# Alternating two blocks' DVE chains between the layers of a two-layer graph network, with the second layer's tables moved to the end of the stage

## What is computed

```python
h = relu(layernorm(x));  x = x + L0_gnn(h, ...)      # 12500 nodes x 160, 212500 edges
h = relu(layernorm(x));  x = x + L1_gnn(h, ...)

# layer 0, end of it: messages summed per node into agg (449 columns, one of them a count)
cnt   = clip(segment_sum(1, dst), 1)
alpha = mean(scal) @ Wa * a * inv96
conv  = [mean(scal) @ Wl2_s, mean(vec) @ Wl2_v] * a * inv96
x     = x + sc + alpha * conv
# layer 1, start of it
h     = relu(layernorm(x))
f, skip = h @ W_nl, h @ W_skip          # features gathered by edge, and a skip path
w     = relu(edge_feature @ W_fc1) @ W_fc2   # one row per edge, 224 columns
sh    = edge_attr / |edge_attr|
# then: gather f by dst, multiply, segment_sum by src, W_out, gate, add
```

## Time and profile before

| what | value |
|---|---|
| median of 3 runs | 9630.93 us (9630.51 to 9639.42) |
| the profiled execution | 9623.72 us |
| its span, first to last instruction | 9622.0 us |
| `middle`, first PE instruction to the next stage's first | 6302.34 to 6991.42 us of the span |
| whole span, busy | PE 72%, DVE 75%, ACT 51%, POOL 72% |

### The profile page before, as it was taken

How to read it: one execution, slowest core, us unless ns; L and a number is a source line. 1 busy time by engine, 2 the same in 40 slices (tenths; PEclk the granted TensorE clock), 3 DMA queues, 4 the chain that set the end, 5 groups by cost and what they waited for, 6 DMA issues and landing times. The chain is left out here.

```text
span 9622.0 us, 170670 instructions
## 1 busy us (share of the span) xinstructions
PE 6909.3 (72%) x31166; PEld 4531.3 (47%) x31166; DVE 7250.6 (75%) x21188; ACT 4950.1 (51%) x16490; POOL 6942.6 (72%) x7069
## 2 busy tenths in 40 slices
PE   5666666655666666666666666668789999999999
PEld 3333333332222222222222222245578888888889
DVE  7565665665777777777777777777789999999995
ACT  3444444443444444444444444434467777777774
POOL 4777777777777777777777777756677777777770
PEclk8655555567888888888888888888899999999999
DMA  2222222224444444444444444445456666666667
GB/s 90 92 92 92 92 91 92 92 90 124 138 138 136 137 138 137 137 136 135 138 137 137 137 138 138 130 138 158 153 159 168 169 168 167 168 171 167 170 166 210
DMA packets 826473, 1315.62 MB, mean 137 GB/s; under 512 B 228520, under 2 KB 627624, under 8 KB 826280
## 3 DMA queue, kind: packets, MB, share of 16 engines
q0 software_dynamic: 337920, 667.48, 24.7%
q1 hardware_dynamic: 417496, 547.30, 18.8%
q10 hardware_dynamic: 70992, 100.14, 3.0%
HBM read 862.45 MB, written 914.08 MB: 185 GB/s over the span
## 5 line engine op out<-in xcount | busy, mean ns | idle before, releaser
L1445 POOL DMA_INDIRECT feat_m<-feat_tab,rows_m x3712 | 3653.1, 984 | 1155.3 <-issue 997.9
L1578 ACT ACTIVATE prod_m<-part_m,rows_m 128x64 f32<-128x64 f32 x5568 | 1432.4, 337 | 2197.5 <-DVE part_m L1768 2141.2
L1545 PE MATMUL pair<-prod_m,hot_m 128*128 128x160 f32 x14848 | 2243.5, 304 | 159.2 <-DVE prod_m L1751 119.7
L1545 PEld LDWEIGHTS pair<-prod_m,hot_m 128*128 128x128 f32 x14848 | 2043.4, 190 | 359.4 <-issue 358.2
L1522 PE MATMUL bank<-prod_m,hot_m 128*128 128x449 f32 x2476 | 1424.3, 709 | 944.6 <-DVE prod_m L1788 795.7
L1566 ACT ACTIVATE hot_m<-hot_m,rows_m 128x128 f32<-128x128 f32 x5568 | 1728.7, 389 | 693.1 <-DVE hot_m L1734 687.9
L652 POOL DMA_INDIRECT sorted_rows<-rows_e,place_e x1664 | 1614.4, 970 | 532.1 <-issue 505.2
L1464 POOL DMA_INDIRECT sorted_rows<-later_m,place_m x1248 | 1262.4, 1012 | 380.4 <-issue 345.3
L1522 PEld LDWEIGHTS bank<-prod_m,hot_m 128*128 128x128 f32 x2476 | 542.7, 241 | 1840.1 <-issue 1629.0
L1751 DVE TENSOR_TENSOR prod_m<-rows_m,feat_m 128x192 f32<-128x192 f32 (+2 forms) x4640 | 1316.4, 323 | 0.0
L1768 DVE TENSOR_TENSOR part_m<-rows_m,feat_m 128x128 f32<-128x128 f32 x928 | 271.1, 292 | 1015.1 <-DMA feat_m<-feat_tab,rows_m 1012.1
(11 more groups left out here) (250 smaller groups left out, 10209.4 us busy)
## 6 DMA issues: line engine op xcount, KB each, us to landing
agg_tab<-acc_m ACTq DMA_DIRECT2D x928, 320.0 KB
rows_m<-sorted_rows SPq DMA_DIRECT2D x928, 229.0 KB
agg_tab<-acc_m ACTq DMA_DIRECT2D x928, 224.5 KB
rows_m<-sorted_rows SPq DMA_DIRECT2D x928, 197.0 KB
feat_m<-feat_tab,rows_m POOLq DMA_INDIRECT x3712
turned_m<-in_turned ACTq DMA_DIRECT2D x159, 256.0 KB
agg_s<-agg_tab SPq DMA_DIRECT2D x98, 320.0 KB, 3.3
sorted_rows<-rows_e,place_e POOLq DMA_INDIRECT x1664, 2.4
```

Source lines behind the costliest of these rows:

```text
L1445: pool.indirect_dma_start(out=feat[s % RING][:, k, :], out_offset=None, in_=g.feat_tab[l.n], in_offset=bass.IndirectOffsetOnAxis(ap=rows[s ...
L1545: mm = pe.matmul(dst, hot[s % l.hot_bufs][:, k, q, :], rhs, start=(k == 0 and col == 0), stop=(k == ST_TILES - 1), skip_group_check=True)
L1578: ins = act.activation(prod[s % prods][:, k, at:at + S0], part[s % 2][:, k, 0:S0], ACT.Copy, scale=rows[s % HELD][:, k, l.sh_at + m:l.sh_a ...
```

## The change

DVE's chain is cut into its links. `add_conv` and `node_stats` are split into `count`, `count_inverse`, `count_scale`, `alpha`, `add_conv` (block of one step back) and `stats`, `aggregate`, `positive` (now of two steps back), and a step issues them in turn. What follows from the statistics comes a step later on every engine: `inverse_root`, `root`, `node_turn`, `node_move`, `node_product`, `finish` and the stores (`BLOCK_LAG` 5 to 6). The tables are made after the last step, and PE waits there until the PSUM banks are free. No instruction is added or taken away apart from waits; the buffers are the same.

```diff
-BLOCK_LAG = 5
+BLOCK_LAG = 6
...
 # tensor
             hidden(0, 0)
-            tables_pe(pe, x, g)
...
-                behind(2, node_turn)(step, it, s)
-                behind(3, node_product)(step, it, s)
+                behind(3, node_turn)(step, it, s)
+                behind(4, node_product)(step, it, s)
             turns(pe, MID_STEPS, DEEP, step_, upto=FULL // DEEP)
+            pe.wait_ge(evicted, MID * 4)
+            pe.wait_ge(x_done, NBLK)
+            pe.wait_ge(feat_ready, NBLK)
+            tables_pe(pe, x, g)
...
 # scalar
-                behind(1, root)(step, it, s)
-                behind(2, node_move)(step, it, s)
-                behind(3, finish)(step, it, s)
+                behind(2, root)(step, it, s)
+                behind(3, node_move)(step, it, s)
+                behind(4, finish)(step, it, s)
...
 # vector
             bin_hot(nc, dve, r, g, 0, 0, None)
-            tables_dve(dve, x, g)
...
             def step_(step, it, s):
                 prepare(step, it, s)
+                behind(1, count)(step, it, s)
+                behind(2, stats)(step, it, s)
+                behind(1, count_inverse)(step, it, s)
+                behind(2, aggregate)(step, it, s)
+                behind(1, count_scale)(step, it, s)
+                behind(1, alpha)(step, it, s)
+                behind(2, positive)(step, it, s)
                 behind(1, add_conv)(step, it, s)
-                behind(1, node_stats)(step, it, s)
-                behind(2, inverse_root)(step, it, s)
+                behind(3, inverse_root)(step, it, s)
             turns(dve, MID_STEPS, DEEP, step_, upto=FULL // DEEP)
+            tables_dve(dve, x, g)
```

More of the change, by code:

```diff
@@ L1291, in prepare, with held, count, stats @@
                                       ALU.mult).then_inc(copied, 1)
-            def add_conv(step, it, s):
+            def held(step, it, s):
                 b = it * DEEP + s
-                c = cnt[s % 2]
+                return b, cnt[s % 2], g.x_sb[:, bass.ds(b, 1), :].rearrange("p o d -> p (o d)")
+            def count(step, it, s):
+                b, c, _ = held(step, it, s)
                 dve.wait_ge(here[s], 16 * (it + 1))
                 dve.tensor_scalar(c[:, 0:1], agg[s][:, L0.ones_at:L0.ones_at + 1], 1.0, None, ALU.max).then_inc(chain, 1)
+            def stats(step, it, s):
+                b, _, xb = held(step, it, s)
+                dve.wait_ge(x_done, b + 1)
+                if step is None or step >= 2:
+                    dve.wait_ge(root_ready, b - 1)
+                    dve.wait_ge(h_ready, b - 1)
+                    settle(dve, g.passed)
+                dve.bn_stats(bn[s % 2][:, :], xb).then_inc(stat, 1)
+            def count_inverse(step, it, s):
+                b, c, _ = held(step, it, s)
                 dve.wait_ge(chain, 4 * b + 1)
                 dve.reciprocal(c[:, 1:2], c[:, 0:1]).then_inc(chain, 1)
+            def aggregate(step, it, s):
+                b, _, _ = held(step, it, s)
+                dve.wait_ge(stat, b * 2 + 1)
+                settle(dve, g.passed)
+                dve.bn_aggr(mv[s % 2][:, :], bn[s % 2][:, :]).then_inc(stat, 1)
+            def count_scale(step, it, s):
+                b, c, _ = held(step, it, s)
                 dve.wait_ge(chain, 4 * b + 2)
                 dve.tensor_tensor(c[:, 2:3], c[:, 1:2], g.attr_s[:, 2, bass.ds(b, 1)], ALU.mult).then_inc(chain, 1)
+            def positive(step, it, s):
+                b, _, xb = held(step, it, s)
+                dve.wait_ge(stat, b * 2 + 2)
+                if step is None or step >= 2:
+                    dve.wait_ge(turn_ready, b - 1)
+                dve.tensor_scalar(node_h[s % 2][:, :], xb, mv[s % 2][:, 0:1], 0.0, ALU.subtract, ALU.max).then_inc(h_ready, 1)
+            def alpha(step, it, s):
+                b, c, _ = held(step, it, s)
                 dve.wait_ge(chain, 4 * b + 3)
@@ L1304, in add_conv @@
                 dve.tensor_scalar(c[:, 3:4], res[:, 160:161], c[:, 2:3], c[:, 2:3], ALU.mult, ALU.mult).then_inc(chain, 1)
+            def add_conv(step, it, s):
+                b, c, _ = held(step, it, s)
                 dve.wait_ge(chain, 4 * b + 4)
@@ L1310, in add_conv @@
                                          ALU.mult, ALU.add).then_inc(x_done, 1)
[L1312 to L1328, removed]
             def inverse_root(step, it, s):
```

## The result

| what | before | after |
|---|---|---|
| median of 6 runs each | 9632.24 us (9622.33 to 9639.42) | 9578.98 us (9571.14 to 9584.22) |
| ratio | 1 | 0.9944, 95% interval 0.9931 to 0.9957 |
| span of the profiled execution | 9622.0 us | 9571.7 us |
| `middle`, first PE instruction to the next stage's first | 689.1 us | 627.9 us |
| from that start to the first send | 34.0 us | 15.8 us |

The change is faster, by 53 us where 120 had been forecast, and the time lies outside the range. The stage itself became 61.2 us shorter in the profiled pair.

A forecast was written before the change was run, and what follows sets the result against it. The prediction took DVE's chain of dependent links, not throughput, to bound `middle`. Terms of -18.3 (tables leaving the start), -103.1 (52 chunks at 10.45 us) and +1.5 (tables at the end) gave -119.9, forecast 9511 us, range 9490 to 9560.

The forecast's parts named there:

- What bounds now: In `middle` no engine is full; a chain limits, with DVE the engine others wait for and its dependent links leaving idle time.
- Tables leave the start: Start of `middle`: tables no longer hold up the first transpose, so all that follows comes 18.3 us earlier.
- A block's chain 3.00 to 1.97: DVE's links of one block: alternating them cuts 3.00 us to 1.97, about 2 us a chunk.
- DVE alone 10.15 a chunk: DVE in `middle`: 9.95 us a chunk after the saving, plus 0.2 us given back waiting for the product.
- POOL's floor 10.1: POOL's eight sends a chunk, each 0.96 us and 0.30 of issue, need 10.1 us.
- What bounds next: Chunk in `middle`: floor 10.1 us, with DVE 10.15, POOL 10.1 and PE with its slab wait 10.6 as limits.
- The clock, 0.35 on top: TensorE's granted clock in `middle` adds 0.35 us a chunk to the floor, between nothing and 0.57, giving 10.45.
- The sum: Whole kernel: -18.3 - 103.1 + 1.5 = -119.9 us, the other four stages unchanged.
- Tables at the end, +1.5: End of `middle`: tables finish 3.6 us behind the last send and cost 1.5 us, bounds 0 and +8.2.
- Steps later for ACT, PE and SP: Their work behind the statistics comes one step later, with the same work and hand-over distances: costed at nothing.
- The slab: Rival in `middle`: PE's slab wait gives 10.6 us a chunk, 8 us more, 9519; clock or slab had chance 0.24.
- the alternation brings nothing: Rival on DVE's links: a chunk stays at 12.43 us, only the tables' -16.8 us remains, 9614; chance 0.09.

The follow-up runs named there:

- a5: Changed kernel with PE's next-chunk counts moved ahead of the odd step's product and SP's slab load ahead of `load_agg`: 9522.06 us, 0.9899 of the kernel before.
- a4: Changed kernel with the previous block's statistics behind the addition instead of between DVE's links, lags and tables kept: 9572.87 us, 0.9954 of the kernel before.
- a1: Kernel before with only the tables moved to the end of the stage: 9608.14 us, 0.9991 of the kernel before.
- b4: Changed kernel with SP's load of the turned slab moved ahead of `load_agg`: 9579.98 us, 0.9960 of the kernel before.

## Why the prediction was wrong

- *What bounds now.* Right as far as it went: DVE's chain and its dependent links. It said of DVE that "what it waits for itself is dealt with next" and then read only the gaps between its links. The line on L340, 26.8 us, went unread, though it is a wait of DVE for PE.
- *Tables leave the start, -18.3.* Measured -18.2 to the first send, -17.8 for the stage with this part alone. Right.
- *A block's chain 3.00 to 1.97.* Measured 1.98. Right, with two terms off that cancel: 0.05 us from `count` to `stats` and 0.22 from `aggregate` to `count_scale`, where 0.12 stood for each. The reading that an independent instruction starts before the one in front of it is over is right too. By the rule weighed there (the Trainium skill, "VectorE: DVE Perf Modes", "The DRAIN you can't avoid", and for the advice to cut instructions the page's "Rules for kernel authors"), the links would have kept their 3.00 us; this trace disagrees with it at 1.98 us for the same ten instructions. The same section adds that an instruction which isn't held starts earlier; with that the trace agrees.
- *DVE alone 10.15 a chunk.* a5 shows 10.18 at full clock. Right, but not reached in the changed kernel.
- *POOL's floor 10.1.* It left out the sends that last longer than 0.96 us: about 23 us of the stage in a5, 0.45 a chunk.
- **What bounds next: this step failed.** It put the floor at 10.1 and named three limits above it, DVE, POOL, and PE with the slab; all are sums of one engine's work. The limit was a loop through two engines: addition, product, the rest of PE's queue, counts, ranking, links. In it DVE's links are 2.0 of 11.18 us. The timeline of before gives the same loop at 10.89 us, already above the floor of 10.1. By the starts that the prediction took for the new order, 0.12 + 0.48 + 0.12 + 0.29 + 0.43 + 0.20 and the 0.34 of L1309 = 1.98 us lie from `count` to the addition's end, so 10.89 - 1.71 + 1.98 = 11.16 us could have been summed. What DVE saves in the odd step lies outside the loop and turns into waiting at L340. In the trace of the changed kernel that wait is 60.7 us.
- *The clock, 0.35 on top.* The sends take 603.5 / 52 = 11.60 us a chunk, 0.42 over the 11.18 of full clock, ends included. The grant rose from 0.89 to 0.93 in the steady stretch; the forecast of above 0.9 held.
- *The sum.* 52 x (11.60 - 10.45) = 60 us is the whole of the miss in the stage: -119.9 + 60 = -60, measured -61.2. Of the 60, 52 x (11.18 - 10.1) = 56 are the floor and the rest the clock. The profiled pair moved by 50.3 us, 61.2 less the 10.9 that the four other stages took longer, and the medians by 53.
- *Tables at the end, +1.5.* Measured 0: they end 3.7 us behind the last send (3.6 forecast), inside the 8.6 us that the stage needs there anyway.
- *Steps later for ACT, PE and SP, costed at nothing.* Not a cost: taken with the statistics' lag on DVE it is a gain, 32.9 us of the stage by a4 against a1. The runs do not part what of this is the moved statistics and what the moved hand-overs; that stays open.
- *The rivals.* The slab was second in line and not what decided (b4); the clock's 0.42 us a chunk is 22 us on top, near the 0.35 forecast. That the alternation brings nothing is wrong for DVE's chain; of this kernel's time only 10.5 us of the stage hang on it, and the median without it (a4) can't be told from the one with it. PE held at 1.2 GHz did not occur: the lowest mean grant of a chunk is 0.72, for single ones.

## What to carry to other kernels

Before forecasting what an engine's shorter chain gives, list every wait of that engine, the small ones above all, and follow each once around: the sum of the loop through the other engines' queues is a floor like an engine's own work. A saving in a stretch that isn't part of the loop turns into waiting in front of it; the same edit was worth 10 us here with the loop in place and 35 to 45 with it broken. An edit that puts new work between the links of the loop makes it longer, even where it shortens the engine's own chain. An instruction in an in-order queue that needs nothing of what stands ahead of it, like PE's counts, is the cheapest place to break one.

## What the runs showed of the hardware

**A send that starts inside L320 waits for its end.** Over the ten kernels with L320 as one instruction, 213 sends start 0.05 to 0.35 us after it does (it lasts 0.99 us, both inputs in SBUF), and all 213 last over 1.3 us in place of 0.96. Looked at by offset, the median send lasts 1.70 us at 0.1 us behind L320's start, 1.53 at 0.3, 1.34 at 0.5 and 1.08 at 0.7: start and duration add up to 1.8 us behind L320's start each time. At 0.9 it has its 0.96 again. The length of DVE's instruction is not the cause: of the 415 sends that start inside L350 (0.99 us, a reduction with one input) and the 583 inside L331 (1.52 us, bf16 as L320 is, one input), none lasts over 0.98 us, and none of the 276 inside L340 (0.99 us, one input in PSUM). A send that has started when L320 starts keeps its 0.96 us in all 285 cases (0.98 at most), and L320 lasts 0.98 to 1.02. The Trainium skill ("SBUF — State Buffer", "SBUF: two separate sides") says that VectorE with two SBUF inputs and a GpSimd instruction that reads SBUF share a port pair as an exclusive lock, and that whoever comes first holds it for the whole instruction. The trace agrees for a send that comes second; it doesn't for one that comes first, since L320 isn't held up by it.

**A chunk's phase decides how often it happens.** 8 of 416 sends were long in the kernel before and 41 in the changed one, though neither engine's instructions changed: at a constant 11.18 us a chunk the same send, the third, meets L320 again and again. The changed kernel's POOL paid 24 us more for it, at a time when it had slack.

**The clock is low in single chunks in every version.** In the changed kernel they take 12 to 14.7 us at a grant of 0.72 to 0.87, in a5 13.25 us at 0.79 with PE busy throughout, between neighbours at 0.94 and 1.00. The mean grant over the steady stretch lies between 0.88 and 0.94 in all kernels here, and no run showed what starts such a chunk.
